# Routed experts: weights of all experts held in SBUF and copied per block by ScalarE, in place of loads from HBM per block

## The reference, cut to what matters

```python
def _L1_ffn_ref(x, Wr, br, W1, b1, W2, b2):      # x: 128 x 96 x 64, 64 experts
    xf = x.reshape(-1, D)
    logits = xf @ Wr + br
    topk_logits, topk_idx = jax.lax.top_k(logits, TOP_K)      # TOP_K = 2
    gates = jax.nn.softmax(topk_logits, axis=1)
    combine = jnp.zeros((T, E), xf.dtype).at[jnp.arange(T)[:, None], topk_idx].add(gates)
    out = jnp.zeros((T, W2.shape[-1]), xf.dtype)
    for e in range(E):
        h = jax.nn.relu(xf @ W1[e] + b1[e])      # 64 -> 128
        y = h @ W2[e] + b2[e]                    # 128 -> 64
        out = out + combine[:, e:e + 1] * y
    return out.reshape(Bx, Sx, -1)

h = h + _L1_ffn_ref(_layernorm(h, axis=-1), ...)
```

## Time and profile before

| | us |
|---|---|
| median of 3 timed runs | 2414.56 (2413.54 to 2418.58) |
| span of the profiled execution | 2525.0 |
| POOL busy with its 256 indirect DMAs of L1422 | 245.2 |
| first and last of these begin at | 2045.52, 2481.10 |

### The profile page before, as it was taken

How to read it: one execution, slowest core, us unless ns; L and a number is a source line. 1 busy time by engine, 2 the same in 40 slices (tenths; PEclk the granted TensorE clock), 3 DMA queues, 4 the chain that set the end, 5 groups by cost and what they waited for, 6 DMA issues and landing times.

```text
span 2525.0 us, 52330 instructions
## 1 busy us (share of the span) xinstructions
PE 1871.0 (74%) x16279; PEld 1453.1 (58%) x16279; DVE 1618.5 (64%) x5056; ACT 979.6 (39%) x3166; POOL 1087.2 (43%) x878
## 2 busy tenths in 40 slices
PE   5788887999999999999996477763333256666661
PEld 2257776777777777777774265552222155555561
DVE  0047773588888888888886799977888612222223
ACT  2277772344444444444442599862121100000000
POOL 0036660233434434344333322214888735555552
PEclk9989996899999999999995588885555555555555
DMA  9910000000000000000000000000000054434426
GB/s 276 292 51 0 0 0 1 2 2 2 1 0 0 0 0 0 0 0 0 0 1 1 0 1 1 1 1 11 23 22 23 24 159 111 115 111 113 114 74 158
DMA packets 119878, 106.65 MB, mean 42 GB/s; under 512 B 62448, under 2 KB 109680, under 8 KB 118896
## 3 DMA queue, kind: packets, MB, share of 16 engines
q1 hardware_dynamic: 87024, 73.88, 11.2%
q10 hardware_dynamic: 18432, 16.79, 2.2%
q0 software_dynamic: 14336, 14.91, 1.8%
HBM read 78.84 MB, written 26.67 MB: 42 GB/s over the span
## 4 chain that ended last, share of the span: by engine, by line
PE 30%; DVE 21%; issue 19%; POOL 11%; another core or an unknown queue 9%; ACT 2%; DMA 1%; DVEq 1%; ACTq 1%; SPq 0%; POOLq 0%
POOL routed_rows L1409 6%; PE PS L654 5%; PE PS L621 3%; PE PS L688 3%; PE PS L669 3%; PE PS L949 2%; POOL rstd L1310 2%; DVE XR L1563 2%; DVE XR L1763 1%; DVE XR L1559 1%; PE PS L941 1%; PE PS L703 1%; PE PS L728 1%; DMA arena<-expert_rows 1%
## 5 line engine op out<-in xcount | busy, mean ns | idle before, releaser
L1038 ACT ACTIVATE arena<-PS 128x384 f32<-128x384 f32 (+4 forms) x400 | 187.6, 486 | 665.4 <-remote 210.9
L1422 POOL DMA_INDIRECT expert_rows<-arena x256 | 245.2, 958 | 214.2 <-DVE arena L1953 141.7
L1943 DVE TENSOR_SCALAR arena<-PS 128x512 f32<-128x512 f32 x64 | 44.2, 691 | 359.8 <-remote 224.5
L1559 DVE TENSOR_REDUCE XR<-PS 128x2 f32<-128x192 f32 (+2 forms) x768 | 173.7, 280 | 105.0 <-PE PS L654 105.0
L654 PE MATMUL PS<-arena 32*128 32x96 f32 (+2 forms) x3072 | 234.1, 285 | 0.0
L1409 POOL DMA_INDIRECT routed_rows<-XR,SLu x192 | 199.7, 1040 | 75.0 <-issue 70.8
L949 PE MATMUL PS<-arena 128*128 128x64 f32 x512 | 126.0, 428 | 141.6 <-DVE arena L1943 140.7
L949 PEld LDWEIGHTS PS<-arena 128*128 128x128 f32 x512 | 114.0, 328 | 168.6 <-DVE arena L1943 142.6
L654 PEld LDWEIGHTS PS<-arena 32*128 32x128 f32 x3072 | 198.4, 192 | 20.7
L1355 POOL TENSOR_TENSOR arena<-arena,mhalf 96x16 f32<-96x16 f32 x32 | 93.3, 2915 | 241.6 <-DVE arena L1605 241.6
L1074 ACT ACTIVATE XR<-PS 128x256 f32<-128x256 f32 x512 | 167.3, 380 | 67.1 <-PE PS L669 66.9
(11 more groups left out here) (306 smaller groups left out, 4633.9 us busy)
## 6 DMA issues: line engine op xcount, KB each, us to landing
arena<-in_x_dram SPq DMA_DIRECT2D x32, 784.0 KB, 9.9
arena<-in_t_experts_dram ACTq DMA_DIRECT2D x128, 128.0 KB
arena<-in_t_experts_dram SPq DMA_DIRECT2D x128, 128.0 KB
routed_rows<-zt SPq DMA_DIRECT2D x16, 528.0 KB, 6.2
arena<-routed_rows SPq DMA_DIRECT2D x64, 132.0 KB
expert_rows<-arena POOLq DMA_INDIRECT x256
WP<-in_t_pack_dram SPq DMA_DIRECT2D x1, 3425.0 KB, 21.3
routed_rows<-XR,SLu POOLq DMA_INDIRECT x192
```

The costliest lines, as they stand in the source:

```text
L1038: return act.activation(dst, src, ACT.Identity, **kw)
L1422: pool.indirect_dma_start(YD, bass.IndirectOffsetOnAxis(yi[:, u % 4, k:k + 1], 0), yb[:, u % 4, k, :], None).then_inc(e_st[u % 2], 16)
L1559: dve.tensor_reduce(negmax[:, p, j, :], PS[:, S_:S_ + 2, S_AT[j]:S_AT[j] + QB * (j + 1)], AX_X, ALU.max, negate=True).then_inc(b_max, 1)
```

## The change

All weights are loaded once into `wall`, 64 experts x 256 f32 a partition, by 8 DMAs that SP issues when the recurrent block is done (`c_h`). `load_weights` on ACT becomes `pick_weights`: for each of the four blocks it reads the expert's number and copies 128x256 elements from `wall` to the ring `wx`, which now has 4 places (`WRING`) and lies in `XR`. `load_blocks` on SP only loads the rows. PE's `e_hidden` waits for a new semaphore, `e_w`. On ACT the row copy has lag 1 in place of 4 and stands ahead of the pick. To make room, four routing tiles (`dxc`, `dsq`, `dxn`, `Lg`) move from `arena` to `XR`, and `Y2g` to the end of `arena`. The array of weights is laid out by partition on the host, a transposition of the input. A semaphore (`mask_set`) is merged into another (`const_set`), outside these stages; this is left out of the diff.

```diff
@@ -37,6 +37,9 @@
 EB = 4
 CH = B // 4
 RING = 8
+WRING = 4
+WX = NHX + 2 * D
+WLOADS = 8
 GD = 8
 NR = B // GD
 GDC = GD * D
@@ -293,12 +296,15 @@
             return td(name, [P, n // 2]).bitcast(BF16)
         OH = [bf(f"OH{u}", 2 * NVX) for u in range(2)]
         OHs = [bf(f"OHs{u}", NVX) for u in range(2)]
-        dxc = td("dxc", [NTOK, 2, GDC])
-        dsq = td("dsq", [NTOK, GDC])
-        dxn = td("dxn", [NTOK, 2, GDC])
+        XG = Arena(XR)("XG", [P, 2, NV, 2, ROW])
+        tdx = Arena(XR)
+        tdx.at = 2 * NV * 2 * ROW
+        dxc = tdx("dxc", [NTOK, 2, GDC])
+        dsq = tdx("dsq", [NTOK, GDC])
+        dxn = tdx("dxn", [NTOK, 2, GDC])
         dxF = td("dxF", [P, 2, 2 * FC])
         dst = td("dst", [NTOK, 2, 4, GD])
-        Lg = td("Lg", [P, 2, NV, NX])
+        Lg = tdx("Lg", [P, 2, NV, NX])
         m8 = td("m8", [P, 2, NV, 8])
         i8 = td("i8", [P, 2, NV, 8]).bitcast(U32)
         TI = td("TI", [P, 2, 2, NV])
@@ -316,15 +322,21 @@
         bex = td("bex", [P, 2])
         SLu = sb("SLu", [P, 2, 2, NV], U32)
         blku = sb("blku", [1, NBLK], U32)
-        XG = Arena(XR)("XG", [P, 2, NV, 2, ROW])
+        tw = Arena(arena)
+        tw.at = 22528 - NX * WX
+        assert td.at <= tw.at
+        wall = tw("wall", [P, NX, WX])
         te = Arena(arena)
         xb = te("xb", [P, RING, EB, ROW])
-        wx = te("wx", [P, RING, EB, NHX + 2 * D])
+        wxr = Arena(XR)
+        wxr.at = B * D - WRING * EB * WX
+        wx = wxr("wx", [P, WRING, EB, WX])
         xT = te("xT", [D + 1, 2, EB * SLOT])
         hT = te("hT", [P, 2, EB * SLOT])
         yb = te("yb", [P, 4, EB, D])
         yi = te("yi", [P, 4, EB]).bitcast(U32)
-        Y2g = te("Y2g", [NTOK, B * D])
+        assert te.at <= tw.at - NX * WX
+        Y2g = arena[0:NTOK, 22528 - B * D:22528]
         zt = sb("zt", [P, 16, ROW])
         wpack = t_in["t_experts"]
         XD = nc.dram_tensor("routed_rows", (NBLK * SLOT, ROW), F32, kind="Internal").ap()
@@ -415,15 +427,17 @@
 
             def load_blocks(g, u):
 
-                wait(sp, e_in[u % 4], (g - u % 4) * (4 * (1 + EB)))
+                wait(sp, e_in[u % 4], (g - u % 4) * 4)
                 sp.sem_inc(go, 1)
                 wait(sp, e_y, g - (RING - 1))
                 sp.dma_start(xb[:, u, :, :], XD[ds(g * (EB * SLOT), EB * SLOT)].rearrange("(k p) d -> p k d", p=P)
                              ).then_inc(e_in[u % 4], 16)
-                for k in range(EB // 2):
-                    e = sp.value_load(blku[0:1, ds(g * EB + k, 1)], min_val=0, max_val=NX - 1)
-                    sp.dma_start(wx[:, u, k, :], wpack[ds(e, 1)].rearrange("o p w -> p (o w)")).then_inc(e_in[u % 4], 16)
-
+
+            sp.wait_ge(c_h, NR)
+            n = NX // WLOADS
+            for c in range(WLOADS):
+                sp.dma_start(wall[:, c * n:(c + 1) * n, :].rearrange("p e w -> p (e w)"),
+                             wpack[:, c * n * WX:(c + 1) * n * WX]).then_inc(weights_in, 16)
             for u in range(2):
                 sp.wait_ge(scat[u], 16 * NR * NV)
             sp.wait_ge(d_blk, 1)
@@ -927,7 +941,7 @@
             pe.wait_ge(d_blk, 3)
 
             def e_transpose(g, u):
-                pe.wait_ge(e_in[u % 4], (g - u % 4) * (4 * (1 + EB)) + 16 * (1 + EB))
+                pe.wait_ge(e_in[u % 4], (g - u % 4) * 4 + 16)
                 wait(pe, e_xTs, g - 1)
                 pe.sem_inc(go, 1)
                 for k in range(EB):
@@ -937,8 +951,10 @@
             def e_hidden(g, u):
                 pe.wait_ge(e_xTs, g + 1)
                 wait(pe, e_h, g - 1)
+                pe.sem_inc(go, 1)
+                pe.wait_ge(e_w, g + 1)
                 for k in range(EB):
-                    mm = pe.matmul(PS[:, 2 + u % 2, k * SLOT:(k + 1) * SLOT], wx[0:D + 1, u, k, 0:NHX],
+                    mm = pe.matmul(PS[:, 2 + u % 2, k * SLOT:(k + 1) * SLOT], wx[0:D + 1, u % WRING, k, 0:NHX],
                                    xT[:, u % 2, k * SLOT:(k + 1) * SLOT], start=True, stop=True)
                 mm.then_inc(e_up, 1)
 
@@ -947,7 +963,7 @@
                 wait(pe, e_y, g - 1)
                 for k in range(EB):
                     mm = pe.matmul(PS[:, 4 + u % 2, k * D:(k + 1) * D], hT[:, u % 2, k * SLOT:(k + 1) * SLOT],
-                                   wx[:, u, k, NHX:NHX + D], start=True, stop=True)
+                                   wx[:, u % WRING, k, NHX:NHX + D], start=True, stop=True)
                 mm.then_inc(e_down, 1)
 
             grouped(pe, NBLK // EB, (0, e_transpose), (2, e_output), (1, e_hidden), unroll=RING)
@@ -1271,20 +1287,18 @@
                 wait(act, e_up, g - 1)
                 copy_out(xT[0:D, u % 2, :], bank(u % 2, D, EB * SLOT)).then_inc(e_xTs, 1)
 
-            def load_weights(g, u):
-
-                wait(act, e_in[u % 4], (g - u % 4) * (4 * (1 + EB)))
+            def pick_weights(g, u):
+
+                wait(act, e_y, g - (WRING - 1))
                 act.sem_inc(go, 1)
-                wait(act, e_y, g - (RING - 1))
-                act.sem_inc(go, 1)
-                for k in range(EB // 2, EB):
+                for k in range(EB):
                     e = act.value_load(blku[0:1, ds(g * EB + k, 1)], min_val=0, max_val=NX - 1)
-                    act.dma_start(wx[:, u, k, :], wpack[ds(e, 1)].rearrange("o p w -> p (o w)")).then_inc(e_in[u % 4], 16)
-
-            for u in range(2):
-                act.wait_ge(scat[u], 16 * NR * NV)
+                    a = act.activation(wx[:, u % WRING, k, :], wall[:, ds(e, 1), :].rearrange("p o w -> p (o w)"), ACT.Identity)
+                a.then_inc(e_w, 1)
+
+            act.wait_ge(weights_in, 32 + 16 * WLOADS)
             act.wait_ge(d_blk, 1)
-            grouped(act, NBLK // EB, (0, load_weights), (4, e_rows), unroll=RING)
+            grouped(act, NBLK // EB, (1, e_rows), (0, pick_weights), unroll=RING)
 
 
         @block.gpsimd
@@ -1949,7 +1963,7 @@
                 link = Link(dve, chain6, g, 1)
                 link.base += 2 * NR + 14 * NR
                 link(dve.tensor_tensor(yb[:, u % 4, :, :], PS[:, 4 + u % 2, 0:EB * D].rearrange("p (k d) -> p k d", k=EB),
-                                       wx[:, u, :, NHX + D:NHX + 2 * D], ALU.add))
+                                       wx[:, u % WRING, :, NHX + D:NHX + 2 * D], ALU.add))
                 dve.tensor_tensor(yb[:, u % 4, :, :], yb[:, u % 4, :, :],
                                   xb[:, u, :, D + 1:D + 2].broadcast_to([P, EB, D]), ALU.mult).then_inc(e_y, 1)
             grouped(dve, NBLK // EB, (1, e_relu), (2, e_out), unroll=RING)
@@ -2101,6 +2115,7 @@
     w1, b1, w2, b2 = (inputs.pop("L1_ffn_" + n) for n in ("W1", "b1", "W2", "b2"))
     pack = np.zeros((NX, P, NHX + 2 * D), np.float32)
     pack[:, 0:D, 0:NHX], pack[:, D, 0:NHX], pack[:, :, NHX:NHX + D], pack[:, :, NHX + D:] = w1, b1, w2, b2[:, None, :]
+    pack = pack.transpose(1, 0, 2).reshape(P, -1)
...
```

More of the change, by code:

```diff
@@ L337, in build @@
         turn_done, turn_kept = sem("turn_done"), sem("turn_kept")
-        const_set, mask_set = sem("const_set"), sem("mask_set")
+        const_set = sem("const_set")
         rows_done, rows_kept = sem("rows_done"), sem("rows_kept")
@@ L359, in build @@
         out_sem = sem("out_sem")
-        (d_lg, d_lgS, d_m8, d_i8, d_top, d_ohs, d_rank, d_rowT, chain6, d_cell, d_slots, d_rows, d_tokc, d_exp, d_diff, d_blkp, d_blk, zt_set, zeros_out, e_xT, e_xTs, e_up, e_h, e_down, e_y, go, d_comb) = map(sem, (
-            "d_lg d_lgS d_m8 d_i8 d_top d_ohs d_rank d_rowT chain6 d_cell d_slots d_rows d_tokc d_exp d_diff d_blkp d_blk zt_set zeros_out e_xT e_xTs e_up e_h e_down e_y go d_comb").split())
+        (d_lg, d_lgS, d_m8, d_i8, d_top, d_ohs, d_rank, d_rowT, chain6, d_cell, d_slots, d_rows, d_tokc, d_exp, d_diff, d_blkp, d_blk, zt_set, zeros_out, e_xT, e_xTs, e_up, e_h, e_down, e_y, go, d_comb, e_w) = map(sem, (
+            "d_lg d_lgS d_m8 d_i8 d_top d_ohs d_rank d_rowT chain6 d_cell d_slots d_rows d_tokc d_exp d_diff d_blkp d_blk zt_set zeros_out e_xT e_xTs e_up e_h e_down e_y go d_comb e_w").split())
         scat = [sem(f"scat{u}") for u in range(2)]
@@ L575, in _ @@
             pe.wait_ge(a_h, NG)
-            pe.wait_ge(mask_set, 2)
+            pe.wait_ge(const_set, 8)
             pe.wait_ge(const_set, 6)
@@ L1300, in _ @@
             pool.wait_ge(weights_in, 32)
-            pool.tensor_copy(cmask[:, :], b_tri[:, :]).then_inc(mask_set, 1)
-            pool.tensor_copy(identb[:, :], ident[:, :]).then_inc(mask_set, 1)
+            pool.tensor_copy(cmask[:, :], b_tri[:, :]).then_inc(const_set, 1)
+            pool.tensor_copy(identb[:, :], ident[:, :]).then_inc(const_set, 1)
             pool.wait_ge(zt_set, 1)
```

## The result

The changed kernel takes 2404.09 us (2396.02 to 2409.92, 8 runs), the kernel before on the same chip 2416.57 us (2413.54 to 2429.04, 8 runs): ratio 0.9943 [0.9923, 0.9964], which is 8.7 to 18.6 us less. The forecast was 2406, 8 us under the 2414.6 that the kernel before had in its three runs; the medians now stand 12.5 us apart.

What follows compares the result with a forecast made beforehand. The prediction took POOL's indirect DMAs, 5.05 us a group, to set the expert stage's pace in the timed runs. 2414.6 - 8 (start of the stage) + 0 = 2406.6, said as 2406 us, range 2399 to 2411.

Steps and rivals of the forecast that it cites:

- the start of the stage: Start of the expert stage: without ACT's ten weight issues ahead of it, the first row copy comes 8 us earlier (4 to 9).
- the chain behind the first copy: Start of the expert stage: 9.68 us from ACT's first row copy to POOL's start, PE's and unchanged.
- the one on the stalls: Expert stage: 110.4 us of stalls in the profile come from the recording; timed runs lack them, so removing loads gains nothing there.
- The equality that I leaned on: Expert-stage stalls of 110.4 us equal the 110.4 us by which the profiled run exceeds the timed median.
- the sign that I named for this reading: Whole kernel: timed median near 2406 us while the profile's span falls by over 100 us, the two nearly meeting.
- Rival B: Expert stage: stalls are real and in timed runs too, removed with the weight loads; 2296 us, 2351 if half; chance 0.14.
- Rival D: Start of the expert stage: the gain there is absent; 2416 us at most, between 2411 and 2419; chance 0.15.
- The picks: ACT, expert stage: four a group at 0.7 us, reads beside copies; 3.6 us a group under POOL's 5.05, nothing added.
- The row in series: ACT, expert stage: if index reads and 493 ns copies ran one after another, the ACT step would be 5.6 us.
- So the wait is over before it starts: ACT, expert stage: a pick's wait for group g-4 costs nothing, as PE is two steps past it, about 9 us.
- The bulk load: After the last write of H: 8.4 MB in eight DMAs, 30 us at 276 GB/s, hidden before the first scatter.
- POOL as the pace: Expert stage: POOL's four indirect DMAs a group, 5.05 us, set the pace in the timed runs.

## Why the prediction was right, and where it was wrong

**The time was right, from the step it was built on.** I forecast 8 us (4 to 9) from the start of the stage. The time fell by 12.5 us (8.7 to 18.6) and by 7.9 at the higher level, so 2404 for the forecast 2406 is closer than the gain is. Against the trace of before at the same level the change gains 23.81 - 15.67 = 8.14 us from last scatter to first send. Block load to transposition took 2029.32 - 2026.74 = 2.58 us where I took 2.5, and the chain behind the first copy 9.74 where I had 9.68.

**One small term was missing.** I costed the sends at nothing. First to last send is 325.0 us in place of 326.7: fewer sends run over 1 us (busy 245.4 in place of 246.6) and one loop turn is 0.5 us shorter. With the 8.14 that is 9.8 us, where the times have 8.7 to 18.6. The tail behind the last send is 43.0 in place of 44.0 us, but it goes from 43.1 to 45.5 in the kernel before and its variants and from 42.9 to 44.1 in the changed ones, so no gain is shown there.

The two spans differ by 6.9 us only, since in this pair the first scatter was 3.6 us later after the change and the last 4.0. That lies ahead of the routing stage: from the last write of `H` in the recurrent block to the first scatter are 30.8 us in each of the fourteen traces, so the moved routing tiles cost nothing, as forecast. In the trace of after, PE's granted clock is 0.66 and 0.65 between 1668 and 1690 and from there to 1713 us, where the trace of before at the same level has 0.84 and 0.90, and the last two writes of `H` stand 12.9 and 10.4 us apart in place of 8.6 and 8.4. The first scatter's time runs from 1729.6 to 1746.5 us over the traces, on average 6 us later in the six with the change. Most of that spread is there by 130 us: the eleventh instruction of DVE begins between 114.0 and 130.0 us. The times show no such loss; whether it is chance is left open.

**The step that failed** is the one on the stalls, "I read this as a slowdown that the recording causes: in the timed runs POOL already sets the pace", in that it set the profile against the timed runs. A recorded execution of the same program had none (span 2415.0), so recording alone does not make them, and timed runs had them (2516 and 2523 us). They belong to a level into which whole comparisons fall. What makes the level, and whether the recording has a part in it, stays open. The first trace of before happened to be taken at the higher level, its three timed runs and the trace of after at the lower. The equality that I leaned on, 110.4 us of stalls against 110.4 us over the timed median, was true and said only that the stalls make up the difference; it did not say why the one execution had them. And the sign that I named for this reading, a timed median near 2406 while the span falls by over 100 us, came true by the same luck. The rule on the recording block, by NOTIFIC, the notification-queue block, of the Trainium skill, section "7.1 Overflow: three behaviours, one of which stalls the engine", is shown at work by no run here.

**Rival B** (the stalls are the loads' and in the timed runs) has half a point: they are in timed runs of the higher level. But the kernel without loads and the changed kernel have them too, and the change gains 100 us at neither level. Rival D fell with the 8.14 us at the start.

**The picks** went as forecast: I had 0.7 us each, the index reads beside the copies (0.75 apart in the list of signs), and they stand 0.65 us apart in the trace. The row in series by ScalarE: Activation LUTs of the Trainium skill, section "What ACT_TABLE_LOAD costs", came to 493 ns a copy; the copy of 128x256 with a register address took 416, and the series did not happen. By that section of the Trainium skill the 493 are for a bias by pointer, and for an immediate scale and bias its figures give the estimate 186 + 0.833 x 256 = 399 ns. The row of 400 agrees with the second.

"So the wait is over before it starts" was wrong: ACT's picks wait 88.6 us in all for group g-4 to be done, 59 times and at most 3.3 us, as the row of L1296 above and the waits show. It costs nothing, because ACT has the room and PE is not held up: ahead of PE's hidden layer hardly any idle time is left, in its matrix products or its weight loads:

```profile
ACT XR L1296 <- DVE arena L1967: 88.6, 59, 3.3
```

```profile
L957 PEld LDWEIGHTS PS<-arena,XR 65*128 65x128 f32 x512 | 116.8, 333 | 0.3 <-issue 0.3
L957 PE MATMUL PS<-arena,XR 65*128 65x128 f32 x512 | 129.4, 434 | 0.0
```

**The bulk load** was hidden, as said, and shorter. Its issues on the timeline, and the moved GB/s between 1700 and 1760 us in 40 slices of 1.5 us:

```profile
1712.97 3.96 SPq L439 DMA_DIRECT2D arena<-in_t_experts_dram  x8
```

```profile
GB/s 0 0 0 0 0 0 0 0 0 147 399 421 431 426 426 437 421 431 404 421 431 431 355 22 0 0 0 0 0 27 24 23 23 0 23 23 23 28 23 23
```

It is over by 1736 us, at some 420 GB/s where I took 276, and the first scatter starts at 1743.1. The scatters, first to last, took 281.4 us after and 281.1 before.

**POOL as the pace** was right: a fifth send costs 76 us, and removing one gives back only what PE's 4.57 us leave.

## What to carry to other kernels

Before you price stalls, ask whether the profile and the times are of the same level: if the span differs from the timed median by more than a few us, get a second trace and the span of each timed run, and don't invent a cause for the difference. Taking traffic off queues that were not the bound gave here little more than what stood in the chain at the start of the stage. One timeline gave that to a few tenths of a us, which is finer than the times can confirm. When you take one late item out of a chain (ACT's ten issues), name the next (SP's weights), and look for circles when an instruction moves ahead of a load.

## What the runs showed of the hardware

- The same program has two levels in its timed runs, 2411 to 2417 us in four comparisons and 2516 to 2523 in two. The chip with number 10 gave 2516.45 once and 2411.24 once. The difference is some 20 to 30 stalls of about 4 us, every 14 to 20 us, in the stretch where POOL issues indirect DMAs back to back. In a stall, waits on several engines end within 0.1 us of each other, and an assert of 18 ns takes 700. No assert takes over 0.3 us in the eight traces of the lower level. What triggers the stalls is open: they come in both kernels, with and without weight loads, and less with three sends a group (25 us in place of 110).
- An indirect DMA of 128 rows costs POOL 1.26 us start to start (0.96 + 0.30) at either level.
- A load of 1 MB per DMA, eight in a row on one queue, ran at some 420 GB/s; ACT copies 128x256 f32 within SBUF in 416 ns with the index read (276 ns) beside it.
